# Second graph layer of a four-layer graph and expert network: row norms a further step later, and the values of three row tiles projected inside the attention

## The chip, the cores and the metric

The kernel runs on one core of one Trainium2 chip. The metric is the device time of one execution in microseconds (us), as the median of several runs; less is better. The engines are named as the profile names them: PE is TensorE's matmul, PEld its weight load, DVE is VectorE, ACT is ScalarE, POOL is GpSimd, SP is SyncE.

## What is computed

Four layers run one after the other on 1024 rows of 256 numbers, all in float32 unless said otherwise. Each layer is a graph step and then a mixture of experts, each added to `x`:

```python
x = x + gnn(layernorm(x), adj, ...)      # a different one in each layer
x = x + ffn(layernorm(x), ...)           # two of 16, 8, 8 or 16 experts a row
```

The change touches the graph step of the second layer (layer 1), an attention with 4 heads of 64 columns over a dense mask:

```python
h = (x @ W.T).reshape(n, 4, 64)                    # the values
e_src = einsum('nhd,hd->nh', h, a_src)
e_dst = einsum('nhd,hd->nh', h, a_dst)
e = leaky_relu(e_src[:, None, :] + e_dst[None, :, :], 0.2)
e = where(adj > 0, e, -inf)
out = einsum('ijh,jhd->ihd', softmax(e, axis=1), h).reshape(n, 256)
```

## The kernel before

The 1024 rows are 8 row tiles of 128 (`NT` is 8, `P` is 128, `D` is 256 in `DC` = 2 parts). Every stage is one block in which each engine has its own instruction list, written out in order; engines wait for each other by semaphores. A block ends when all engines have ended, and the next starts on all of them.

**The stage before the attention** is the end of the first layer's expert block, class `BeforeGraph1`. DVE sums a row tile, norms it twice (`summed`, `raised`, `norm`); PE turns it (`turn`, L196), ACT places the turned tile in `xnT` (`place`, L201), and PE projects it (`project`, L1004): the destination terms of 4 heads (L1012), the values (L1018), the source terms (L1020). ACT copies the three results out of PSUM in `keep` (L1030, L1033, L1034). PE's order is turn of tile t, then project of tile t-1. The weights' products stand in `w`, `wa`, `wab`; the values go to `V`.

**The attention** is `graph1` (L1093). It goes in 32 units; unit u is head u % 4 of row tile u // 4. For one unit:

- DVE: `mask` (L443) adds the mask row block to the destination terms and takes the row maximum, 128x1024;
- POOL: three small operations on 128x1 (L482, L483, L485) make two biases of the maximum; the third gives `biased`;
- ACT: `slope_of` (L498) applies slope and bias, 128x1024, and gives `sloped`;
- DVE: `shift` (L451) combines both branches into `lm`, 128x1024;
- PE: `turn` (L537) transposes `lm` in 8 parts; ACT: `exp_of` (L507) takes the exponential in two halves; PE: `weigh` (L548) multiplies by `V`, 8 parts.

The orders are loops over a step u, the same number on each engine:

```python
DVE  step u: mask(u); shift(u-2); end(u-behind); vector_step(u)     # L462
POOL step u: three operations of unit u; pool_step(u)               # L479
ACT  step u: exp_of(u-3); slope_of(u); scalar_step(u)               # L516
PE   step u: turn(u-2); weigh(u-3); tensor_step(u)                  # L555
```

`behind` is 5 here. `end` does something for every fourth unit only: `finish` of a whole row tile (L1104 to L1106).

**Beside the attention** the norm and the gate logits of each finished row tile are worked into these steps by `attend` (L569) with the class `Front`: DVE takes the `moments` (L238 to L242), POOL takes the power (`invert`, L250), DVE writes the normed tile (`norm`, L187), PE turns it (L196), ACT places it (L201), PE makes the `logits` (L262), DVE ranks them (`rank`: L273, L281, L282). The step of each is counted from `done(t)` = 4t+8, where the moments of row tile t stand. With `wait` = `behind` - 4 = 1 they are, before the change: the power at step 4t+9, norm and turn at 4t+10 and 4t+11, place 4t+12, logits 4t+13, rank 4t+14. What falls behind the last step is done in `vector_end`, `tensor_end`, `scalar_end` and `pool_end`. The same function serves the first layer (behind 4, wait 0) and the fourth (behind 4, wait 0).

SP loads the gate's weights and stores the normed tiles in DRAM while this runs; POOL issues no DMA in this block.

Of the kernel before, what the change touches and what calls it, by code (L numbers as in the profile page):

```python
# [15 lines left out]
P = 128  # L16
N = 1024
NT = N // P
D = 256
# [7 lines left out]
def build(nc, A, out):  # L27
# [19 lines left out]
    with top:  # L47
# [361 lines left out]
        def attention(block, ph, heads, slope, lowest, rows, rest, values, width, finish,  # L409
# [81 lines left out]
            @block.scalar  # L491
            def _(act):

                def slope_of(u):
                    act.wait_ge(biased, u + 1)
                    if u >= 4:
                        act.wait_ge(shifted, u - 3)
                    nc.scalar.activation(t2[u % 4][:, :], g[u % 4][:, :], ACT.Identity, bias=b2[:, u:u + 1],  # L498
                                         scale=slope).then_inc(sloped, 1)

                def exp_of(u):
                    for hf in range(2):
                        act.wait_ge(turned, 2 * u + hf + 1)
                        if u >= 2 and hf == 0:
                            act.wait_ge(weighed, u - 1)
                        q = slice(hf * NT // 2, (hf + 1) * NT // 2)
                        nc.scalar.activation(pT[u % 2][:, q, :], tp[u % deep][:, q, :], ACT.Exp)\  # L507
                            .then_inc(exped, 1)

                ahead = 1  # L510
                slope_of(0)
                if "scalar_early" in extra:
                    slope_of(1)
                    extra["scalar_early"](act)
                    ahead = 2
                for u in range(ahead, units + 3):  # L516
                    if u >= 3:
                        exp_of(u - 3)
                    if u < units:
                        slope_of(u)  # L520
                    if "scalar_step" in extra:
                        extra["scalar_step"](u, act)
                if "scalar_end" in extra:
                    extra["scalar_end"](act)
# [42 lines left out]


        def attend(block, ph, front, heads, slope, lowest, rows, rest, values, width, finish, scores, done, free=0,  # L569
                   settle=None, more=(), group=1, behind=4):  # L570

            units = NT * heads
            wait = behind - 4

            def normed(t):
                return done(t) + 1 + wait
# [88 lines left out]

            def pool_step(u, pool):
                for t in range(NT):  # L670
                    if done(t) + wait == u:
                        front.invert(pool, t)

            def pool_end(pool):
                for t in range(NT):
                    if done(t) + wait >= units:
                        front.invert(pool, t)

            def sync(sp):
# [3 lines left out]
            hooks = {"vector_step": vector_step, "vector_end": vector_end, "tensor_step": tensor_step,  # L683
                     "tensor_end": tensor_end, "scalar_step": scalar_step, "scalar_end": scalar_end,
                     "pool_step": pool_step, "pool_end": pool_end, "sync": sync}
            for name in ("tensor", "scalar_early"):
                if name in more:
                    hooks[name] = more[name]
            attention(block, ph, heads, slope, lowest, rows, rest, values, width, finish, scores, hooks, group, behind)
# [234 lines left out]


        class BeforeGraph1(Handover):
            H, DH, SLOPE = 4, 64, 0.2
            base = xn


# [73 lines left out]
            def project(self, pe, t):  # L1004
                H = self.H
                q = slice(t * P, (t + 1) * P)
                pe.wait_ge(self.norm.xnT_ready, t + 1)
                if t >= 2:
                    pe.wait_ge(self.columns_kept, t - 1)
                for h in range(H):  # L1010
                    for c in range(DC):
                        ins = nc.tensor.matmul(self.pd[t % 2][:, h, :], self.wab[:, c, h, :], xnT[:, c, q],  # L1012
                                               start=(c == 0), stop=(c == DC - 1))
                ins.then_inc(self.columns, 1)
                if t >= 2:
                    pe.wait_ge(self.values_kept, t - 1)
                for c in range(DC):
                    nc.tensor.matmul(self.pv[t % 2][:, 0:D], xnT[:, c, q], self.w[:, c, :], start=(c == 0), stop=(c == DC - 1))  # L1018
                for c in range(DC):
                    ins = nc.tensor.matmul(self.pv[t % 2][:, D:D + H], xnT[:, c, q], self.wa[:, c, :],  # L1020
                                           start=(c == 0), stop=(c == DC - 1))
                ins.then_inc(self.valued, 1)

            def scalar(self, act):
                H, DH, SLOPE = self.H, self.DH, self.SLOPE
                nc.scalar.activation(spent[:, :], power[:, 0, :], ACT.Exp)

                def keep(t):
                    act.wait_ge(self.columns, t + 1)
                    nc.scalar.activation(self.dst[:, :, t * P:(t + 1) * P], self.pd[t % 2][:, :, :], ACT.Copy)\  # L1030
                        .then_inc(self.columns_kept, 1)
                    act.wait_ge(self.valued, t + 1)
                    nc.scalar.activation(self.rest[:, t, :], self.pv[t % 2][:, D:D + H], ACT.Copy, scale=1.0 - SLOPE)  # L1033
                    nc.scalar.activation(self.V[:, t, :, 0:DH], self.pv[t % 2][:, 0:D].rearrange("p (h d) -> p h d", h=H),  # L1034
                                         ACT.Copy).then_inc(self.values_kept, 1)
                for t in range(NT + 1):
                    if t < NT:
                        self.norm.place(act, t)
                    if t >= 1:
                        keep(t - 1)  # L1040
# [52 lines left out]
        def graph1(before, gate_of):  # L1093
            H, DH, SLOPE = before.H, before.DH, before.SLOPE
            rest, dst, V = before.rest, before.dst, before.V
            with Phase("g1") as ph:
                r, part = ph.sb("r", [P, NT, H, 1]), [ph.sb(f"part{n}", [P, H, DH]) for n in range(2)]
                tp = ph.ps("front_tp", [P, DC, P])
                psl = ph.ps("front_psl", [P, NT, gate_of[0]])
                front = Front(ph, *gate_of, [tp[:, :, :]], psl, raised_here=range(NT))  # L1100
                block = ph.block()

                def finish(t, dve, link, o, gm):
                    link(nc.vector.reciprocal(r[:, t, :, :], o[:, :, DH:DH + 1]))  # L1104
                    link(nc.vector.tensor_tensor(part[t % 2][:, :, :], o[:, :, 0:DH], bc(r[:, t, :, :], [P, H, DH]), ALU.mult))
                    return nc.vector.tensor_tensor(x[:, t, :], x[:, t, :], part[t % 2][:, :, :].rearrange("p h d -> p (h d)"),  # L1106
                                                   ALU.add)

                attend(block, ph, front, H, SLOPE, lambda u: False, lambda u: dst[:, u % H, :],
                          rest[:, :, :].rearrange("p t h -> p (t h)"),  # L1110
                          lambda u, c: V[:, c, u % H, :], DH + 1, finish, None, lambda t: (t + 1) * H + 4, group=H, behind=5)


        class BeforeGraph2(Handover):
# [1120 lines left out]
```

## Time and profile before

| what | value |
| --- | --- |
| median of 3 runs | 1093.96 us (1091.34 to 1099.96) |
| the profiled execution's own time | 1096.7 us |
| its span, first to last instruction | 1094.8 us |
| PE busy | 956.3 us (87%) |
| PEld busy | 896.3 us (82%) |
| DVE busy | 701.8 us (64%) |
| ACT busy | 514.7 us (47%) |
| POOL busy | 445.4 us (41%) |
| attention of layer 1, first mask to last moments | 252.16 to 365.5 us |

The span is what the profiler saw between the first and the last instruction; the profiled execution took 1.9 us more than its span and 2.7 us more than the median. Busy time says how long an engine worked, not whether the others waited for it. The trace gives for each instruction its start, its duration and what ended the idle time before it.

### The profile page before, as it was taken

To read this page: it belongs to the slowest core of one execution; us is meant where nothing else is said; L and a number is where in the kernel's file an instruction comes from. 1 tells how busy PE (TensorE), PEld (TensorE's weight loads), DVE (VectorE), ACT (ScalarE), POOL (GpSimd) and SP (SyncE) were. 2 spreads that over 40 slices of the span, in tenths; PEclk is the share of its full clock that TensorE was granted. 3 is DMA by queue.
4 is the path that set the end of the run, shared out by engine and by line. 5 is a ranking of instruction groups with operands and counts; after the bars stand their busy time and mean duration, and the time that the engine had idled before them with its cause. 6 is when DMAs were issued, how large, how long until landed. Compare 5 with 4: busy or idle time off the path is not lost. (4 is left out here: it accounts for less than half of the span.)

```text
span 1094.8 us, 22761 instructions
## 1 busy us (share of the span) xinstructions
PE 956.3 (87%) x7554; PEld 896.3 (82%) x7554; DVE 701.8 (64%) x1653; ACT 514.7 (47%) x1001; POOL 445.4 (41%) x470
## 2 busy tenths in 40 slices
PE   6884999896899589989989899999889985999992
PEld 5584999786888579978979899999758875999992
DVE  3786777666899557776544466655656864666664
ACT  1252777134666357712045577767234532444341
POOL 1152577426776147621200145551244521344441
PEclk8797999798999789979989999999899995999997
DMA  7007865300000437322450011168200007655954
GB/s 250 2 25 241 312 219 178 97 1 1 11 10 11 183 109 269 135 83 95 129 195 8 16 35 38 38 220 308 92 2 5 11 21 268 255 168 172 322 162 135
DMA packets 57675, 132.30 MB, mean 121 GB/s; under 512 B 9664, under 2 KB 35712, under 8 KB 52864
## 3 DMA queue, kind: packets, MB, share of 16 engines
q1 hardware_dynamic: 47376, 106.45, 27.7%
q0 software_dynamic: 9024, 24.65, 7.4%
q8 instruction: 43, 0.70, 0.3%
q10 hardware_dynamic: 1200, 0.23, 0.1%
q14 instruction: 32, 0.26, 0.1%
HBM read 191.97 MB, written 17.56 MB: 191 GB/s over the span
## 5 line engine op out<-in xcount | busy, mean ns | idle before, releaser
L1959 PE MATMUL r_pH<-e_xsT,e_w 128*128 128x128 f32 x2304 | 281.5, 280 | 10.0 <-DVE e_xsT L2072 5.0
L1959 PEld LDWEIGHTS r_pH<-e_xsT,e_w 128*128 128x128 f32 x2304 | 272.4, 197 | 12.8 <-issue 9.6
L1914 POOL DMA_INDIRECT y_rows<-e_ys,e_to x94 | 156.8, 1668 | 190.6 <-DVE e_ys L2102 95.5
L1924 POOL DMA_INDIRECT e_xs<-xn_rows,e_idx x94 | 103.4, 1100 | 161.7 <-DVE e_idx L2076 120.4
L2088 DVE TENSOR_TENSOR e_w_lo<-e_w,e_w_hi 128x1024 fp32r<-128x1024 f32 (+1 forms) x74 | 113.4, 1532 | 13.8 <-ACT e_w_hi L2030 12.7
L1974 PE MATMUL r_pY<-e_w_hi,e_h_hi 128*128 128x256 f32 x384 | 114.5, 298 | 2.2 <-issue 2.2
L2030 ACT ACTIVATE e_w_hi<-e_w 128x1024 fp32r<-128x1024 f32 (+1 forms) x74 | 96.0, 1298 | 27.7 <-DMA e_w<-w_in 22.4
L498 ACT ACTIVATE g_t<-g_g,g_small 128x1024 f32<-128x1024 f32 x56 | 64.1, 1150 | 94.8 <-POOL g_small L485 94.8
L1974 PE MATMUL r_pY<-e_w_lo,e_h_hi 128*128 128x256 f32 x384 | 108.4, 282 | 0.0
L1974 PE MATMUL r_pY<-e_w_hi,e_h_lo 128*128 128x256 f32 x384 | 108.4, 282 | 0.0
L451 DVE SCALAR_TENSOR_TENSOR g_lm<-g_g,g_small,g_t 128x1024 f32<-128x1024 f32 x56 | 71.6, 1280 | 9.5 <-ACT g_t L498 7.0
L537 PE MATMUL g_tp<-ident,g_lm 128*128 128x128 f32 x448 | 62.8, 286 | 16.7 <-DVE g_lm L451 16.0
L1974 PEld LDWEIGHTS r_pY<-e_w_hi,e_h_hi 128*128 128x128 f32 x384 | 73.3, 191 | 2.7 <-issue 2.6
L482 POOL TENSOR_SCALAR g_small<-g_small,n_rest 128x1 f32<-128x1 f32 x48 | 49.5, 1032 | 59.1 <-DVE g_small L443 58.5
L1974 PEld LDWEIGHTS r_pY<-e_w_lo,e_h_hi 128*128 128x128 f32 x384 | 73.5, 191 | 0.0
L1974 PEld LDWEIGHTS r_pY<-e_w_hi,e_h_lo 128*128 128x128 f32 x384 | 73.2, 191 | 0.0
L537 PEld LDWEIGHTS g_tp<-ident,g_lm 128*128 128x128 f32 x448 | 53.0, 149 | 23.6 <-DVE g_lm L451 21.0
L2042 ACT ACTIVATE xnT<-r_pH,e_w 128x128 f32<-128x128 f32 x176 | 50.2, 368 | 44.2 <-PE r_pH L1959 39.0
L548 PE MATMUL g_o<-n_V,g_pT 128*128 128x65 f32 x512 | 62.9, 277 | 5.4 <-ACT g_pT L507 5.3
L548 PEld LDWEIGHTS g_o<-n_V,g_pT 128*128 128x128 f32 x512 | 60.6, 194 | 8.5 <-ACT g_pT L507 7.7
L443 DVE CUSTOM_DVE_ANT_0 g_g<-n_dst,neg 128x1024 f32<-128x1024 f32 x48 | 58.1, 1217 | 13.9 <-PEq L2152 13.9
L179 POOL TENSOR_SCALAR mean_var<-mean_var 128x1 f32<-128x1 f32 x37 | 17.7, 478 | 120.6 <-DVE mean_var L239 81.8
(321 smaller groups left out, 1970.6 us busy)
## 6 DMA issues: line engine op xcount, KB each, us to landing
e_w<-w_in SPq DMA_DIRECT2D x56, 1024.0 KB
e_w<-w_in SPq DMA_DIRECT2D x84, 512.0 KB
e_w<-w_in SPq DMA_DIRECT2D x52, 514.0 KB
e_w<-w_in SPq DMA_DIRECT2D x24, 1028.0 KB
e_w<-y_rows SPq DMA_DIRECT2D x32, 256.0 KB, 5.4
p_adj<-adj_in SPq DMA_DIRECT2D x8, 512.0 KB, 11.3
xn_rows<-xn SPq DMA_DIRECT2D x32, 128.0 KB, 1.7
n_adjT<-adjT_in SPq DMA_DIRECT2D x8, 512.0 KB, 4.9
```

Of the source, the lines that this page charges most:

```text
L443: nc.vector.tensor_tensor_reduce(out=g[u % 4][:, :], in0=rows(u), in1=neg[:, u // heads, :], scale=1.0, scalar=-3e38, op0=ALU.add, op1=ALU ...
L451: nc.vector.scalar_tensor_tensor(out=lm[u % 2][:, :], in0=g[u % 4][:, :], scalar=b1[:, u:u + 1], in1=t2[u % 4][:, :], op0=ALU.add, op1=ALU ...
L498: nc.scalar.activation(t2[u % 4][:, :], g[u % 4][:, :], ACT.Identity, bias=b2[:, u:u + 1], scale=slope).then_inc(sloped, 1)
L537: ins = nc.tensor.transpose(tp[u % deep][:, c, :], lm[u % 2][:, c * P:(c + 1) * P], ident[:, :])
L548: ins = nc.tensor.matmul(o[k % 2][:, part, 0:width], pT[u % 2][:, c, :], values(u, c), start=(c == 0), stop=(c == NT - 1))
L1914: pool.indirect_dma_start(out=y_rows[:, :], in_=ys[b][:, :], in_offset=None, out_offset=bass.IndirectOffsetOnAxis(ap=to[b][:, :], axis=0))\
L1924: pool.indirect_dma_start(out=xs[b][:, :], out_offset=None, in_=xn_rows[:, :], in_offset=bass.IndirectOffsetOnAxis(ap=idx[b][:, :], axis=0))\
L1959: ins = nc.tensor.matmul(pH[b % 2][:, f, :], w1[b][:, at:at + P], xsT[b % 2][:, c, :], start=(c == 0), stop=(c == DC - 1))
L1974: ins = nc.tensor.matmul(pY[m][:, :], h[m][:, f, :], w[m][:, f * D:(f + 1) * D], start=(f == 0 and n == 0), stop=(f == FC - 1 and n == 2))
L2030: nc.scalar.activation(w2_hi[b % 2][:, :], w2[b][:, :], ACT.Copy).then_inc(w2_rounded, 1)
L2042: ins = nc.scalar.activation(hT[b % 2][:, f, :], pH[b % 2][:, f, :], function, bias=b1)
L2088: nc.vector.tensor_tensor(w2_lo[b % 2][:, :], w2[b][:, :], w2_hi[b % 2][:, :].bitcast(F32), ALU.subtract).then_inc(w2_split, 1)
```

## The change

Two things change in layer 1, and the first layer and the fourth keep their steps.

1. In `attend` the number `wait` is given by the caller: 2 for layer 1, 0 for the others. The power stays at step 4t+9 (`power_at` is min(wait, 1)); norm, turn, place, logits and rank of every row tile go one step later, to 4t+11, 4t+12, 4t+13, 4t+14 and 4t+15.
2. The values of row tiles 5, 6 and 7 are no longer projected by `project` and copied by `keep` before the attention. PE does it as its first work in the attention's block (`project` in `graph1`), and ACT copies them to `V` (`place`) ahead of `slope_of(0)`, by the new hook `scalar_first`. Each goes through one of two PSUM banks, `spare`, which afterwards serve as the front's turning space and as the space for the logits.

```diff
@@ attention
                 ahead = 1
+                if "scalar_first" in extra:
+                    extra["scalar_first"](act)
                 slope_of(0)
@@ attend
-                   settle=None, more=(), group=1, behind=4):
+                   settle=None, more=(), group=1, behind=4, wait=0):
...
-            wait = behind - 4
+            power_at = min(wait, 1)
 
             def normed(t):
                 return done(t) + 1 + wait
...
-                    if done(t) + wait == u:
+                    if done(t) + power_at == u:
                         front.invert(pool, t)
...
-                    if done(t) + wait >= units:
+                    if done(t) + power_at >= units:
                         front.invert(pool, t)
@@ BeforeGraph1
-            H, DH, SLOPE = 4, 64, 0.2
+            H, DH, SLOPE, EARLY = 4, 64, 0.2, 5
...
-                for c in range(DC):
-                    nc.tensor.matmul(self.pv[t % 2][:, 0:D], xnT[:, c, q], self.w[:, c, :], start=(c == 0), stop=(c == DC - 1))
+                if t < self.EARLY:
+                    self.values(self.pv[t % 2][:, 0:D], t)
...
+            def values(self, pv, t):
+                for c in range(DC):
+                    ins = nc.tensor.matmul(pv, xnT[:, c, t * P:(t + 1) * P], self.w[:, c, :], start=(c == 0), stop=(c == DC - 1))
+                return ins
+
+            def keep_values(self, pv, t):
+                return nc.scalar.activation(self.V[:, t, :, 0:self.DH], pv.rearrange("p (h d) -> p h d", h=self.H), ACT.Copy)
...
+                    ins = nc.scalar.activation(self.rest[:, t, :], self.pv[t % 2][:, D:D + H], ACT.Copy, scale=1.0 - SLOPE)
+                    if t < self.EARLY:
+                        ins = self.keep_values(self.pv[t % 2][:, 0:D], t)
+                    ins.then_inc(self.values_kept, 1)
@@ graph1
+                spare = [ph.ps(f"front{n}", [P, 512]) for n in range(2)]
+                late, late_kept = ph.sem("late"), ph.sem("late_kept")
+
+                def project(pe):
+                    for t in range(before.EARLY, NT):
+                        if t >= before.EARLY + 2:
+                            pe.wait_ge(late_kept, t - before.EARLY - 1)
+                        before.values(spare[t % 2][:, 0:D], t).then_inc(late, 1)
+                    pe.wait_ge(late_kept, NT - before.EARLY)
+
+                def place(act):
+                    for t in range(before.EARLY, NT):
+                        act.wait_ge(late, t - before.EARLY + 1)
+                        before.keep_values(spare[t % 2][:, 0:D], t).then_inc(late_kept, 1)
...
-                          lambda u, c: V[:, c, u % H, :], DH + 1, finish, None, lambda t: (t + 1) * H + 4, group=H, behind=5)
+                          lambda u, c: V[:, c, u % H, :], DH + 1, finish, None, lambda t: (t + 1) * H + 4,
+                       more={"tensor": project, "scalar_first": place}, group=H, behind=5, wait=2)
```

## Rows read from the trace of the kernel before

**Rows 1.** Waits of DVE, 252 to 370 us: who waited for whom, us, times, longest

```profile
DVE xn L187 <- POOL rstd L250: 6.3, 7, 1.0
DVE lg L273 <- PE g_front_psl L262: 5.7, 2, 3.6
DVE g_lm L451 <- ACT g_t L498: 5.1, 3, 1.9
```

**Rows 2.** Timeline of one row tile (start, duration, engine, line): DVE, POOL, ACT, steps 16 to 19

```profile
296.74 0.41 DVE L187 TENSOR_SCALAR xn<-x,mean_var,rstd 128x256 f32<-128x256 f32 x1 [0.97 <-POOL rstd L250]
...
305.89 0.38 ACT L201 ACTIVATE xnT<-g_front_tp 128x256 f32<-128x256 f32 x1
...
306.15 1.09 ACT L507 ACTIVATE g_pT<-g_tp 128x512 f32<-128x512 f32 x2
...
306.57 1.22 DVE L443 CUSTOM_DVE_ANT_0 g_g<-n_dst,neg 128x1024 f32<-128x1024 f32 x1
...
307.72 1.28 DVE L451 SCALAR_TENSOR_TENSOR g_lm<-g_g,g_small,g_t 128x1024 f32<-128x1024 f32 x1
307.94 1.21 POOL L483 TENSOR_SCALAR g_small<-g_small 128x1 f32<-128x1 f32 x1
309.23 0.19 POOL L485 TENSOR_TENSOR g_small<-g_small,n_rest 128x1 f32<-128x1 f32 x1
...
309.97 0.42 DVE L187 TENSOR_SCALAR xn<-x,mean_var,rstd 128x256 f32<-128x256 f32 x1 [0.97 <-POOL rstd L250]
...
310.85 1.21 DVE L443 CUSTOM_DVE_ANT_0 g_g<-n_dst,neg 128x1024 f32<-128x1024 f32 x1
```

**Rows 3.** Timeline of steps 7 and 8, before the first norm: DVE, POOL and PE

```profile
270.99 1.28 DVE L451 SCALAR_TENSOR_TENSOR g_lm<-g_g,g_small,g_t 128x1024 f32<-128x1024 f32 x1
...
271.21 2.27 POOL L483 TENSOR_SCALAR g_small<-g_small 128x1 f32<-128x1 f32 x1
...
272.19 1.22 DVE L443 CUSTOM_DVE_ANT_0 g_g<-n_dst,neg 128x1024 f32<-128x1024 f32 x1
...
274.97 1.29 DVE L451 SCALAR_TENSOR_TENSOR g_lm<-g_g,g_small,g_t 128x1024 f32<-128x1024 f32 x1 [1.55 <-ACT g_t L498]
...
275.47 0.77 PE L548 MATMUL g_o<-n_V,g_pT 128*128 128x65 f32 x5 [0.56 <-ACT g_pT L507]
```

**Rows 4.** Timeline of the stage's end (row tile 5, then 7) and the attention's first mask

```profile
242.15 1.03 PE L1018 MATMUL e_pv<-n_w,xnT 128*128 128x256 f32 x4
...
243.02 0.50 PE L1020 MATMUL e_pv<-n_wa,xnT 128*128 128x4 f32 x4
...
249.92 0.17 ACT L1033 ACTIVATE n_rest<-e_pv 128x4 f32<-128x4 f32 x1 [0.61 <-PE e_pv L1020]
249.99 0.38 ACT L1034 ACTIVATE n_V<-e_pv 128x256 f32<-128x256 f32 x1
...
252.16 1.23 DVE L443 CUSTOM_DVE_ANT_0 g_g<-n_dst,neg 128x1024 f32<-128x1024 f32 x1 [12.44 <-PEq L2152]
```

**Rows 5.** ACT's first slopes; then a window: us, busy PE, PEld, DVE, ACT, POOL, PEclk, DMA

```profile
256.45 2.19 ACT L498 ACTIVATE g_t<-g_g,g_small 128x1024 f32<-128x1024 f32 x2 [6.08 <-POOL g_small L485]
...
253.00:254.00 1.00, 0.00 (x0) 0.00 (x0) 1.00 (x3) 0.00 (x0) 0.49 (x1) 1.00 0.17 10
```

**Rows 6.** Timeline of the attention's end: last shift, turn, weigh, logits and finish

```profile
355.93 1.28 DVE L451 SCALAR_TENSOR_TENSOR g_lm<-g_g,g_small,g_t 128x1024 f32<-128x1024 f32 x1
...
358.48 1.04 PE L537 MATMUL g_tp<-ident,g_lm 128*128 128x128 f32 x8
...
359.36 1.90 PE L548 MATMUL g_o<-n_V,g_pT 128*128 128x65 f32 x16
...
361.09 0.56 PE L262 MATMUL g_front_psl<-g_front_gw,xnT 128*128 128x8 f32 x4
...
361.51 1.98 PE L548 MATMUL g_o<-n_V,g_pT 128*128 128x65 f32 x16
...
363.53 0.18 DVE L1104 RECIPROCAL g_r<-g_o 128x4 f32<-128x4 f32 x1 [1.19 <-PE g_o L548]
```

More of the change, by code:

```diff
@@ L685, in attend @@
                      "pool_step": pool_step, "pool_end": pool_end, "sync": sync}
-            for name in ("tensor", "scalar_early"):
+            for name in ("tensor", "scalar_early", "scalar_first"):
                 if name in more:
@@ L1032, in keep @@
                     act.wait_ge(self.valued, t + 1)
-                    nc.scalar.activation(self.rest[:, t, :], self.pv[t % 2][:, D:D + H], ACT.Copy, scale=1.0 - SLOPE)
-                    nc.scalar.activation(self.V[:, t, :, 0:DH], self.pv[t % 2][:, 0:D].rearrange("p (h d) -> p h d", h=H),
-                                         ACT.Copy).then_inc(self.values_kept, 1)
+                    ins = nc.scalar.activation(self.rest[:, t, :], self.pv[t % 2][:, D:D + H], ACT.Copy, scale=1.0 - SLOPE)
+                    if t < self.EARLY:
+                        ins = self.keep_values(self.pv[t % 2][:, 0:D], t)
+                    ins.then_inc(self.values_kept, 1)
                 for t in range(NT + 1):
@@ L1097, in graph1 @@
                 r, part = ph.sb("r", [P, NT, H, 1]), [ph.sb(f"part{n}", [P, H, DH]) for n in range(2)]
-                tp = ph.ps("front_tp", [P, DC, P])
-                psl = ph.ps("front_psl", [P, NT, gate_of[0]])
-                front = Front(ph, *gate_of, [tp[:, :, :]], psl, raised_here=range(NT))
+                spare = [ph.ps(f"front{n}", [P, 512]) for n in range(2)]
[10 more added lines that the diff above has]
+                        before.keep_values(spare[t % 2][:, 0:D], t).then_inc(late_kept, 1)
+                front = Front(ph, *gate_of, [spare[0][:, 0:DC * P].rearrange("p (c q) -> p c q", q=P)],
+                              spare[1][:, 0:NT * gate_of[0]].rearrange("p (t e) -> p t e", e=gate_of[0]), raised_here=range(NT))
                 block = ph.block()
```

## Prediction, made before the changed kernel was run

> **What bounds the kernel now.** I read the engine totals, then the windows of 200 to 370 us, the waits of each engine in the attention, and last the timeline there, instruction by instruction. The totals do not help: PE is busy 87% of the span, but in the changed stretch PE waits and DVE sets the pace. The waits of DVE show three things: it waits for POOL's power before the norm of 7 row tiles, 6.3 us together; three times for a slope, 5.1 us; twice, at the end, for logits [rows 1]. The first is what moving the norm addresses.
>
> The timeline of one row tile shows the period: norm to norm 309.97 - 296.74 = 13.23 us [rows 2]. DVE goes on with its next instruction 1.20 us after a shift starts, so it could have begun at 307.72 + 1.20 = 308.92; the norm starts at 309.97, 1.05 us late. The period is 12.18 us of DVE work and this wait. From the second finished row tile on it repeats unchanged, six times (row tiles 0 to 5; tile 6 waits 0.46 us).
>
> The reader should then look at POOL beside DVE. Its three operations of a unit are 128x1 and take 0.2 to 0.4 us when DVE is idle or small, but L483 at 307.94 takes 1.21 us: it ends 0.15 us after the shift, when DVE has stopped to wait for the norm [rows 2]. L485 follows at once, in that same pause, and the slope of unit 17 can start. So the wait of 1.05 us is also the gap through which POOL gets its result out. What happens without such a gap stands in the steps before the first norm: L483 starts 0.22 us behind a shift, exactly as at 307.94, but a mask follows the shift without a pause; now it takes 2.27 us, until that mask has ended too. The next shift, which needs the slope, comes 274.97 - 272.19 = 2.78 us after that mask, against 307.72 - 306.57 = 1.15 when nothing is missing: DVE stands still for 1.63 us [rows 3]. The same pattern stands once more at 262.54 us, with 1.56 us of waiting by the trace's own count.
>
> **The change, part by part.**
>
> *Values out of the stage before.* The last three row tiles there are PE's: DVE has ended its last norm at 239.7 us and PE works through projections without a gap. From the start of the value matmuls to the start of the next group is 243.02 - 242.15 = 0.87 us [rows 4], three times 2.61 us; tiles 5, 6 and 7 are just the three that PE does back to back. Nothing takes the place: the copies PE waits for (the destination terms, the turned tile) lie over 1 us ahead of its need even at the shorter pace. ACT's last copy goes as well: its end at 249.99 + 0.38 = 250.37 becomes the end of L1033, 249.92 + 0.17 = 250.09 [rows 4], 0.28 us. The attention's first mask came 1.79 us after ACT's end and keeps this distance. Gain 2.89 us; 2.6 if PE's end decides the block's end, 3.1 with the matmuls' full 1.03 us each.
>
> *Values into the attention.* PE does the three tiles from the block's start, ACT copies each in 0.38 us. PE needs 3 x 0.87 = 2.6 us, the last copy ends at about 3.1 us. ACT's first slope starts 256.45 - 252.16 = 4.29 us after the first mask, since POOL's first operation is held up by three masks, and PE's first turn comes later still [rows 4, 5]. So the work is hidden, with 1.2 us to spare: cost 0. The cover is the granted clock: it reads 1.00 until 254 us, 4 us after PE's last matmul in the old stage [rows 5], and PE now pauses about 2 us only. Were it at half, 1.2 GHz, the matmuls would take 5.2 us and the first slope would be 1.1 to 1.9 us late, with the whole attention behind it. The semaphore waits of PE and ACT hold up nothing else, as both wait here for POOL anyway. A turn at a higher clock in the first units gains nothing, since POOL and DVE bound there.
>
> *Norm and what follows, a step later.* Take row tile 2 and lay the new order on rows 2. Until the shift of unit 16 at 307.72 all is as before. Then:
> 1. No norm stands in step 18, so mask 19 starts at 308.92 instead of 310.85. POOL's L483 of unit 17, started at 307.94, sees the shift followed by a mask, the case of rows 3: it ends at 310.2 instead of 309.15. Then L485, slope 17, and only then shift 17: at 308.92 + 2.78 = 311.70, which is 1.63 us later than DVE could.
> 2. Norm 2 stands behind this shift, at 312.90. The power has long been there (POOL takes it in the pause), so the old wait of 1.05 us is gone. The norm takes 0.33 us to the next instruction.
> 3. Then rank 1, now in step 19. It needs logits 1, which stand in PE's step 18 behind weigh 15, behind the exponential of unit 15, which ACT issues behind slope 17, the late one. In rows 3 weigh starts 275.47 - 274.97 = 0.50 us after the late shift. Here place 1 stands between, which has moved to the same step: 306.15 - 305.89 = 0.26 us [rows 2]. So weigh 15 at 312.46; a weigh takes 1.73 us to the next, logits 0.56 us [rows 6]: ready at 314.75, and DVE is there at 313.23. It waits 1.55 us, with the semaphore. Then rank takes 0.55 and mask 20 starts.
> In the finish and in this second pause POOL catches up, so the next step's slopes are in time, and the pattern starts again.
>
> Period: 12.18 + 1.63 + 1.55 = 15.36 us against 13.23, that is 2.13 us more for each row tile. Counted over the attention: shift waits at units 9, 13, 17, 21, 25, 29, six times 1.63 = 9.8 us; rank waits for row tiles 0 to 4, five times 1.55 = 7.75 us; removed, six norm waits of 1.05 = 6.3 us. The last shift is 11.2 us later. I laid all 32 units out in this way, all engines in order; the old order laid out so puts the last finish within 0.2 us of the trace, and the new one gives 11.1.
>
> Bounds: the shift wait lies between 0, if L483 got through at the shift's end, and the 1.9 us of the largest such wait [rows 1]; the two cases with the same neighbours say 1.56 and 1.63. The rank wait lies between 0 and the 3.6 us at the end [rows 1]; it is worked out from ACT's and PE's written order.
>
> *The end.* Before, PE was behind: the last shift ended at 357.21 and its turn started at 358.48, and from shift end to the end of the last weigh it was 363.49 - 357.21 = 6.28 us, with logits 5 between [rows 6]. Now PE has caught up: turn 0.97, two weighs of 1.73 make 4.5 us, 1.75 less. But logits 5 now follow the last weigh, and rank 5 stands ahead of the last finish on DVE: 0.56 + 0.55 = 1.1 us, which nothing hides, since everything after hangs on this finish. The norm of tile 6 is early in either order. Sum of the end: -0.65 us.
>
> Sum for the attention: 11.2 - 0.65 = 10.6 us; with the stage before, 10.6 - 2.9 = **+7.7 us**. What follows the attention starts later by as much, and its work is the same. The profiled execution would take 1096.7 + 7.7 = 1104.4 us; it stood 2.7 us above the median, so for the median 1093.96 + 7.7 = **1101.7 us**.
>
> The Trainium skill, SBUF — State Buffer, section Who interferes with whom, says that a DVE instruction with two SBUF inputs and a GpSimd instruction that reads SBUF exclude each other, and the second blocks until the first has finished. The trace agrees that it blocks, but one POOL instruction lasted through two DVE instructions, 2.27 us [rows 3]. By the page alone L483 would end with the shift and L485 would be caught by mask 19: the slope comes some 0.1 us earlier, and the sum is 1 us less, an estimate by that page.
>
> **The rivals.**
>
> A. *It works as meant.* POOL gets through at the shift's end though a mask follows; L485 also slips in before mask 19. Then the norm waits go, 6.3 us, no rank is late, and with the 2.9 us it is -9.2: 1084.8 us. For it: every such row in the steady part is short (1.21 us). Against it: in all of them DVE is idle or in small operations behind the shift, and both cases without that took 2.27 us. It decides if L483 stays at 1.2 us and L485 at 0.2. This is the case on the other side.
>
> B. *The shift wait comes, the rank wait does not*, because the exponential is ready earlier than I take it. Then 9.8 - 6.3 = 3.5, the end -0.65, the stage before -2.9: about 0, 1093.9 us. Against it: ACT's order is fixed, exponential u-3 behind slope u-1.
>
> C. *The placed values delay the first slope*, at half clock: 1.1 to 1.9 us more, some 1103.2 us. Against it: the clock's row above. A similar price, up to 2 us, would come if PE in its longer pauses (up to 2.2 us) fell to the lower clock for a while; nothing in this trace fell in so short a pause.
>
> **How the numbers follow.** Forecast 0.68, A 0.10, B 0.12, C 0.10. About 1% of the time, 10.9 us, is what a measurement of this kernel can tell from no change (three runs lay 8.6 us apart). Slower by more begins at 1104.9 us: a part of C, and of the forecast what the runs' own spread carries over it, together 0.18. Faster by more begins below 1083.0: less than half of A, 0.04. The rest is 0.78. The range goes from 1089, which takes in B and its spread and leaves out A, to 1107, which takes in C and both waits at 1.9 us; about 0.18 is left out.
>
> **What would show it.** Right: the wait of the norm for POOL is gone; in its place DVE waits for ACT's slope about 8 or 9 times (now 3), near 15 us in sum, and for the logits (L273) some 7 times, 8 us or more beside the last ones. Six more L483 rows at about 2.27 us. First mask near 249.3 us. Norm to norm 15.4 us. PE idle ahead of weigh 2 us once a row tile. L1104's last start follows rank 5 directly. Wrong: a period near 12.2 us with L483 still at 1.2 us (A), a period near 13.8 (B), or a first slope later than 4.3 us behind the first mask (C).

## The result, and the profile after

The changed kernel takes 1107.13 us, the median of 4 runs (1102.55 to 1112.86), the kernel before 1093.88 beside it: ratio 1.012, 95% interval 1.0085 to 1.0155, or +13.2 us where +7.7 was forecast. It is slower, for the reasons forecast and one more. The time lies just outside the range, 0.13 us above its upper end. In the timelines below, rows that stand between those shown are left out.

Waits of DVE in the changed attention, 248 to 378 us (us in total, times, longest), where before had [rows 1]:

```profile
DVE lg L273 <- PE g_front L262: 18.1, 6, 4.5
DVE g_lm L451 <- ACT g_t L498: 14.4, 9, 1.9
DVE xn L187 <- POOL rstd L250: 0.5, 1, 0.5
```

The wait of the norm for the power is gone but for one, as the change meant. The wait for the slope has come nine times instead of three, as forecast. The wait for the logits was to be some 8 us beside the last; it is 18.1 - 4.5 = 13.6 us.

The pattern of one row tile, timeline with PE's clock up (steps 13 to 15; start, duration, engine, line):

```profile
291.00 2.27 POOL L483 TENSOR_SCALAR g_small<-g_small 128x1 f32<-128x1 f32 x1
291.98 1.22 DVE L443 CUSTOM_DVE_ANT_0 g_g<-n_dst,neg 128x1024 f32<-128x1024 f32 x1
293.35 0.19 POOL L485 TENSOR_TENSOR g_small<-g_small,n_rest 128x1 f32<-128x1 f32 x1
294.75 1.29 DVE L451 SCALAR_TENSOR_TENSOR g_lm<-g_g,g_small,g_t 128x1024 f32<-128x1024 f32 x1 [1.55 <-ACT g_t L498]
295.53 2.00 PE L550 MATMUL g_o<-n_V,g_pT 128*128 128x65 f32 x16 [2.05 <-ACT g_pT L507]
295.97 0.40 DVE L187 TENSOR_SCALAR xn<-x,mean_var,rstd 128x256 f32<-128x256 f32 x1
297.97 0.17 DVE L273 TENSOR_TENSOR lg<-g_front,g_front_gb 128x8 f32<-128x8 f32 x1 [1.59 <-PE g_front L262]
```

This is the forecast's pattern in its own numbers. L483, 1.21 us in [rows 2], now lasts 2.27 us as in [rows 3]; it ends with the mask, L485 and the slope follow, and the shift starts 294.75 - 291.98 = 2.77 us behind the mask. The norm stands right behind it, with no wait, and the rank waits 1.59 us, because the weighing ahead of its logits started late. PE paused 2.05 us.

Then comes what was not in the sum. Windows of the same stretch (busy PE, PEld, DVE, ACT, POOL, granted clock, DMA), and PE's and DVE's rows in it:

```profile
300.00:305.00 5.00, 3.64 (x32) 3.27 (x31) 4.83 (x10) 2.12 (x3) 2.70 (x4) 1.00 0.01 2
305.00:310.00 5.00, 4.73 (x23) 4.73 (x23) 3.70 (x6) 0.93 (x1) 4.72 (x6) 0.52 0.00 0
310.00:315.00 5.00, 5.00 (x26) 5.00 (x25) 1.62 (x2) 4.51 (x8) 2.07 (x5) 0.50 0.09 30
...
325.00:330.00 5.00, 5.00 (x29) 5.00 (x29) 3.41 (x5) 2.54 (x5) 4.74 (x7) 0.59 0.00 0
330.00:335.00 5.00, 5.00 (x48) 5.00 (x48) 1.56 (x6) 3.85 (x6) 0.57 (x3) 1.00 0.09 30
```

```profile
305.27 1.97 PE L539 MATMUL g_tp<-ident,g_lm 128*128 128x128 f32 x8 [1.23 <-DVE g_lm L451]
307.04 3.51 PE L550 MATMUL g_o<-n_V,g_pT 128*128 128x65 f32 x16
311.47 0.40 DVE L187 TENSOR_SCALAR xn<-x,mean_var,rstd 128x256 f32<-128x256 f32 x1
316.36 0.17 DVE L273 TENSOR_TENSOR lg<-g_front,g_front_gb 128x8 f32<-128x8 f32 x1 [4.49 <-PE g_front L262]
329.88 0.41 DVE L187 TENSOR_SCALAR xn<-x,mean_var,rstd 128x256 f32<-128x256 f32 x1
333.66 0.17 DVE L273 TENSOR_TENSOR lg<-g_front,g_front_gb 128x8 f32<-128x8 f32 x1 [3.37 <-PE g_front L262]
347.16 0.40 DVE L187 TENSOR_SCALAR xn<-x,mean_var,rstd 128x256 f32<-128x256 f32 x1
```

PE paused 2.05, 0.40 and 1.23 us between its groups; then the granted clock fell from 1.00 to 0.50 (2.4 to 1.2 GHz) and stayed there for some 24 us, although PE was now busy throughout. A turn takes 1.97 instead of 1.04 us, a weighing 3.51 instead of 1.90 [rows 6], and the rank waits of DVE are 4.49 and 3.37 us. The five inside the attention are 1.59, 4.49, 3.37, 1.59 and 2.50 us, 13.5 together. Norm to norm is 15.50 us where the rank between them waits 1.59 us (295.97 to 311.47), and 18.41 and 17.28 where it waits 4.49 and 3.37.

At the stage's end and the attention's start:

```profile
248.04 2.83 PE L1028 MATMUL g_front<-n_w,xnT 128*128 128x256 f32 x12 [2.11 <-PEq L2177]
248.08 1.23 DVE L443 CUSTOM_DVE_ANT_0 g_g<-n_dst,neg 128x1024 f32<-128x1024 f32 x1 [9.73 <-PEq L2177]
250.90 0.39 ACT L1032 ACTIVATE n_V<-g_front 128x256 f32<-128x256 f32 x1 [0.48 <-PE g_front L1028]
252.36 1.15 ACT L498 ACTIVATE g_t<-g_g,g_small 128x1024 f32<-128x1024 f32 x1 [1.08 <-POOL g_small L485]
```

The first mask comes 10.14 us behind the last norm of the stage before; it was 12.85. The last value is copied at 251.29 and the first slope starts 4.28 us behind the mask, as before (4.29, [rows 4, 5]).

Two measures serve below. The **stretch** runs from the attention's first mask to the end of its last moments: 113.3 us before, 130.3 after. The **low clock** is what one-microsecond windows of it show, each counted as 2 x (1 - granted clock), from 12 us behind the first mask on, since PE starts at the lower level in every kernel, to some 2 us before the stretch's end: 0.8 us before, 31.5 after. This count also takes in a first rise that comes late, which is no fall; a table at the end of the experiments tells the two apart. Stretch (+17.0) and stage end (-2.7) make +14.2; the profiled pair differs by 10.6 only, since the other stages, which the change does not touch, took 3.6 us less in it. "Laid out" means all engines' instructions in written order with the durations of the rows, at the full clock; it gives 113.4 for before and 124.1 for after. So 6.2 us of the changed stretch are to be explained, and the clock is the suspect.

### The profile page after: what moved, and what is told of

It is laid out like the page before. It is cut to its first block and busy times, and to the rows that moved or that the text cites. A ratio compares the mean times of both kernels' runs of the same rounds, so it can differ in the third digit from the quotient of the medians.

```text
span 1105.4 us, 22762 instructions
## 1 busy us (share of the span) xinstructions
PE 965.5 (87%) x7554; PEld 904.9 (82%) x7554; DVE 702.4 (64%) x1653; ACT 515.4 (47%) x1001; POOL 448.2 (41%) x470
## 3 DMA queue, kind: packets, MB, share of 16 engines
q1 hardware_dynamic: 47376, 106.45, 27.3%
## 5 line engine op out<-in xcount | busy, mean ns | idle before, releaser
L2113 DVE TENSOR_TENSOR e_w_lo<-e_w,e_w_hi 128x1024 fp32r<-128x1024 f32 (+1 forms) x74 | 113.5, 1534 | 13.2 <-ACT e_w_hi L2055 12.2
L539 PE MATMUL g_tp<-ident,g_lm 128*128 128x128 f32 x448 | 68.7, 304 | 15.1 <-DVE g_lm L451 14.4
L539 PEld LDWEIGHTS g_tp<-ident,g_lm 128*128 128x128 f32 x448 | 58.7, 161 | 22.2 <-DVE g_lm L451 15.2
L550 PE MATMUL g_o<-n_V,g_pT 128*128 128x65 f32 x512 | 70.4, 298 | 6.5 <-ACT g_pT L507 6.4
L550 PEld LDWEIGHTS g_o<-n_V,g_pT 128*128 128x128 f32 x512 | 69.5, 218 | 7.7 <-ACT g_pT L507 7.7
L507 ACT ACTIVATE g_pT<-g_tp 128x512 f32<-128x512 f32 x112 | 60.6, 594 | 12.9 <-PE g_tp L539 12.8
```

What stands on the lines that cost most here:

```text
L539: ins = nc.tensor.transpose(tp[u % deep][:, c, :], lm[u % 2][:, c * P:(c + 1) * P], ident[:, :])
L550: ins = nc.tensor.matmul(o[k % 2][:, part, 0:width], pT[u % 2][:, c, :], values(u, c), start=(c == 0), stop=(c == NT - 1))
L2113: nc.vector.tensor_tensor(w2_lo[b % 2][:, :], w2[b][:, :], w2_hi[b % 2][:, :].bitcast(F32), ALU.subtract).then_inc(w2_split, 1)
```

## The experiments

**The two parts apart.** Values early alone, norms where they were; and norms later alone, with all eight value tiles in the stage before and nothing placed in the attention:

```
e1:  - group=H, behind=5, wait=2)      + group=H, behind=5, wait=1)
e2:  - EARLY = ... 5                   + EARLY = ... 8
```

> Only the values of row tiles 5 to 7 move into the attention; norms, logits and ranks stay at their old steps. The stretch read is from DVE's first mask to its last moments (113.3 us before, 130.3 us changed). Theory T (DVE loses by the steps of norm and rank alone; the moved values are hidden): the stretch stays 113.3 within 0.3 us, the first mask comes 2.9 us earlier relative to DVE's last norm of the old stage, the time falls by 2.9 us to a ratio of about 0.997. Rival R1 (the values in the attention, their PSUM banks or their copies ahead of the first slope cost part of the loss): the stretch is several us longer than 113.3 and the time is not below before.

> Only the norms and all behind them go a step later; all values are projected before the attention as before. T: shift waits of about 1.55 us at six units and rank waits of 1.6 us or more at five, a stretch of 124.2 us if TensorE's granted clock stays at its upper level, and up to 130 us where it falls as in the changed kernel; first mask at its old distance. R1: the stretch is near 113.3 or below, since the values are not there. The intended effect (norm waits gone, nothing in their place) would give 107 us.

Values alone: 1091.90 us (10 runs), ratio 0.9981 (0.9960 to 1.0002), stretch 113.84, low clock 0.0. Norms alone: 1114.86 us (one run), stretch 135.4, low clock 37.5, rank waits up to 8.2 us; this stretch is 5 us over the 130 expected, as the clock fell three times instead of twice, and the third time the last rank waited 8.2 us. The loss is all in the norms. In the profile of the first, PE happened to be at the lower level when it did the placed values:

```profile
246.94 4.51 PE L1028 MATMUL g_front<-n_w,xnT 128*128 128x256 f32 x12 [2.11 <-PEq L2177]
251.49 0.38 ACT L1032 ACTIVATE n_V<-g_front 128x256 f32<-128x256 f32 x1 [1.11 <-PE g_front L1028]
251.77 3.22 ACT L498 ACTIVATE g_t<-g_g,g_small 128x1024 f32<-128x1024 f32 x3
```

4.51 us against 2.83: the first slope comes 4.79 us behind the mask, 0.5 late. That is rival C in small; it is not what made the change slow.

**PE's pause filled.** The changed kernel, with 26 small matmuls (into an unused part of PSUM, issued by the helper `rouse`) ahead of the weighing that waits 2 us; then the same kernel timed:

```
+ def pause(u):
+     if 10 <= u < NT * H and u % H == 2:
+         rouse(spare[1][:, 3 * P:4 * P], 26)
```

> The changed kernel, and in PE's long pause (ahead of weigh in step 4t+10) 26 small bf16 matmuls into an unused part of a PSUM bank, 1.4 us of the 2 us. T with the clock as second cause: the granted clock stays at its upper level from 265 us on, the rank waits are 1.6 us each in place of 1.6 to 4.5, shift waits unchanged at 1.55, the stretch 124.2 us, so some 6 us shorter than the changed kernel's 130.3. Rival R2 (the clock falls for another reason than PE's pauses, or it costs nothing since DVE bounds): dips remain or the stretch stays near 130.

> The kernel of e3 again, now timed: the changed kernel with 26 small matmuls in PE's long pause. One look gave a stretch of 125.1 us and one short fall of the clock. T: with the clock held up most of the time the loss is that of the written order alone, 10.6 - 2.9 = 7.7 us, and what short falls are left add under 1.5 us: time 1102 us, ratio 1.006 to 1.009, clearly under the changed kernel's 1.012. R2 (the clock's falls cost nothing in the time): ratio 1.012 as before the filling.

```profile
302.69 1.09 PE L539 MATMUL g_tp<-ident,g_lm 128*128 128x128 f32 x8 [1.22 <-DVE g_lm L451]
...
306.23 1.61 PE L144 MATMUL g_front<-ones_b 128*128 128x128 bf16 x26
308.44 2.00 PE L550 MATMUL g_o<-n_V,g_pT 128*128 128x65 f32 x16 [0.60 <-ACT g_pT L507]
```

The pause shrinks from 2.05 to 0.60 us and nothing useful is added, yet in the first execution the stretch is 125.1 us and the low clock 8.0: four of the five rank waits are 1.59 to 1.60, one 1.99. The laid out 124.1 is nearly met. Timed, it is 1102.49 us (4 runs), ratio 1.0095 (1.0065 to 1.0125); the profile of that run shows 17.7 us at the lower level and a stretch of 129.2. Of the 17.7 us, 10.8 are the first rise, which came 22 us behind the first mask instead of 13: DVE waited there for two turns, and its first norm comes 2.0 us later than in e3's profile. Only 6.8 us are a fall, at 309.3, right behind the other pause, 1.22 us before a turn, which is left unfilled; the rank behind it waits 4.05 us. Both profiles of this kernel thus show one fall of 6.8 us, the changed kernel's two falls of 30.7 together. The ratio is below the changed kernel's 1.0120, but the intervals overlap: that the time gains by the filling is not shown, the gain in the clock is.

**PE's pauses alone.** The reverse: norms and ranks in the old order, values early, and unused DVE work behind the shift of steps 9, 11, up to 29, that makes PE wait longer.

```
+ for n in range(4):
+     nc.vector.bn_stats(out=gap[...], in_=before.w[:, 0, :])
- wait=2)                     + wait=1)
```

> The kernel with the early values and the norms and ranks of the kernel before (whose stretch was 113.8 us with no lowered clock), with PE's pauses alone made longer: four unused statistics of VectorE, about 1.4 us, behind the shift of every second step from 9 to 29, eleven times, so that PE waits that much longer for the next shifted tile. Nothing of the order of norms and ranks is changed. Theory (the granted clock falls where PE's pauses reach 1.2 to 2.2 us): more than 15 us of the stretch at the lower level, and a stretch over the 123 to 129 us that eleven times 1.35 us on 113.8 give with up to six times 1.0 us of norm waits absorbed. Rival (the clock fell with the later norms and ranks, or by chance, and PE's pauses have nothing to do with it): under 5 us at the lower level, stretch 123 to 129 us.

PE's rows, then windows:

```profile
289.10 1.09 PE L539 MATMUL g_tp<-ident,g_lm 128*128 128x128 f32 x8 [1.32 <-DVE g_lm L451]
...
303.87 1.97 PE L539 MATMUL g_tp<-ident,g_lm 128*128 128x128 f32 x8 [1.45 <-DVE g_lm L451]
305.63 3.52 PE L550 MATMUL g_o<-n_V,g_pT 128*128 128x65 f32 x16
```

```profile
300.00:305.00 5.00, 3.55 (x29) 3.42 (x28) 4.86 (x12) 2.76 (x5) 2.62 (x6) 0.86 0.00 2
305.00:310.00 5.00, 5.00 (x25) 5.00 (x25) 2.84 (x6) 2.90 (x4) 1.82 (x4) 0.50 0.09 30
310.00:315.00 5.00, 5.00 (x25) 5.00 (x25) 4.93 (x12) 2.34 (x3) 1.70 (x3) 0.50 0.00 0
```

Low clock 32.0 us, against 0.0 for the same order without the pauses; stretch 130.4, 1102.32 us (one run). No norm or rank moved, so the rival that ties the clock to their order falls; e1 and e2 show that it is not the moved values either. The pause at 289.10 left the clock up and the like one at 303.87 did not: a pause of this length makes the fall possible, not certain. Longer pauses and less work for PE in each us come together here, and this run can't tell which of the two counts.

**The ranks later.** The rank waits for logits placed only one step before it; `rank_at = logits_at(k) + lag` moves it by `lag` steps. First lag 3 in the changed kernel:

```
- return logits_at(k) + 1             + return logits_at(k) + lag
```

> The changed kernel with every rank two further steps later (step 4t+17), behind the shift that before had only a mask behind it. T: the logits are long there, so no rank waits inside the steps; the 0.55 us of small DVE work now stands in a stretch of masks and shifts and lets POOL catch up, so the shift waits at units 17, 21, 25, 29 shrink from 1.55 to 0.3 us or less; PE's pauses stay under 0.5 us and the clock stays up. Stretch 110.6 us, the time 1094 - 2.9 - 2.7 = 1088, ratio 0.995. If only the rank waits matter and POOL's hold-up is no matter of small work behind a shift, the stretch is 116 to 117 us and the ratio about 1.000.

1097.80 us (10 runs), ratio 1.0027 (1.0001 to 1.0054). No rank waits are left inside the attention, where they took 13.5 us, and the stretch is 8.5 us shorter; but it is 121.8, not 110.6, with a low clock of 32.0 us, 27.3 of it in two falls, one right behind the pause of 2.05 us that this order keeps. DVE now waits for PE's turns (7.9 us, 6 times) and weighings (7.6, 5 times) instead. The expectation of the stretch missed by the clock, which I had taken to matter only for the rank waits, and by something that e8 shows without it.

**Ranks later and pauses filled**, lag 2 (as e3, `lag=2`), lag 3 (fills in steps 4, 7, 10 and 14), and lag 2 timed:

> The changed kernel with every rank one more step later (step 4t+16), where the logits have been ready, and 26 small matmuls in PE's pause. T: the rank waits vanish, five times 1.6 us, the shift waits of 1.55 at six units stay; the last rank no longer stands ahead of the last finish: stretch 116.8 us if the clock holds (124.1 - 7.4). If the rank waits were only the place where another delay shows, the time comes back in the finish or a mask and the stretch stays near 124.

> The kernel of e4 (ranks in step 4t+17) with small matmuls in PE's pauses of the first steps (26 each in steps 4, 10 and 14, 8 in step 7). e4's stretch was 121.8 us, with the clock at its lower level for some 15 us early and 10 us late. T: with the early pauses filled the clock holds and the stretch is the 110.6 to 111.5 us of the written order; time 1094 - 2.9 - 2.5 = 1088.6, ratio 0.995. R2 (falls of the clock have nothing to do with PE's pauses): a stretch of 115 us or more again, ratio 1.00.

> The kernel of the one look at 1088.29 us again, timed: norms at 4t+11, ranks two steps behind the logits (4t+16), 26 or fewer small matmuls ahead of the weighing at the pause. Theory: rank waits stay gone and the shift waits of 1.2 to 1.55 us stay; stretch 116.8 us by the written order, so 1094 - 2.7 + 3.5 = 1094.8 at most and 1088 to 1095 over runs, ratio 0.995 to 1.001. Rival (the clock falls as in the unfilled kernels): stretch over 122 us, time over 1099.

Lag 2: stretch 116.7 us with a low clock of 5.1, as laid out (116.8), 1088.29 us in one run; timed 1092.46 (10 runs), ratio 0.9984 (0.9956 to 1.0012), and there 118.9 with 10.6. In both profiles all of this is the late first rise: with the rank waits gone and the pause filled PE never waits over 0.60 us behind it, and the clock never falls. Lag 3: 1090.66 us (12 runs), ratio 0.9976 (0.9954 to 0.9998), stretch 116.6 and not 110.6. The low clock is 14.2 us, 7.4 of it the first rise; the rest is two falls of 3.4 us behind pauses of 1.45 us in steps that were not filled, and DVE waits for PE in neither. What made the stretch longer is mainly this:

```profile
308.19 1.28 DVE L451 SCALAR_TENSOR_TENSOR g_lm<-g_g,g_small,g_t 128x1024 f32<-128x1024 f32 x1
308.49 1.14 POOL L483 TENSOR_SCALAR g_small<-g_small 128x1 f32<-128x1 f32 x1
309.39 0.41 DVE L187 TENSOR_SCALAR xn<-x,mean_var,rstd 128x256 f32<-128x256 f32 x1
309.72 1.26 POOL L485 TENSOR_TENSOR g_small<-g_small,n_rest 128x1 f32<-128x1 f32 x1
312.19 1.28 DVE L451 SCALAR_TENSOR_TENSOR g_lm<-g_g,g_small,g_t 128x1024 f32<-128x1024 f32 x1 [1.26 <-ACT g_t L498]
```

The later rank freed the step that the expectation named, but behind the norm of the same row tile L483 passes and L485 is held by the next mask, so that the shift after it waits. That comes four times, 1.25 to 1.33 us each, 5.1 us together, and e4 has two of them.

**The held POOL instruction.** If L483 is caught because a mask follows the shift at once, some DVE work in between that leaves POOL alone must let it through. One statistic of 0.43 us behind the shift of step 4t+10, then two, with 12 small matmuls in PE's pause:

```
+ nc.vector.bn_stats(out=gap[...], in_=before.w[:, 0, :])
+ rouse(spare[1][:, 3 * P:4 * P], 12)
```

> The changed kernel with one idle-making DVE instruction (a bn_stats of 0.43 us with one input, result unused) behind the shift of step 4t+10, where only a mask followed, and 12 small matmuls in PE's pause. T (POOL's operation passes as soon as a shift is followed by something that is not a mask): L483 at units 9, 13, 17, 21, 25, 29 takes 1.2 us in place of 2.27, the shift waits there fall from 1.55 to about 0.15 us though DVE has 0.43 us more to do, rank waits stay 1.6: stretch 118.2 us if the clock holds, 5.9 us shorter than 124.1 by an added instruction. Rival (the shift is late for another reason, ACT's order or POOL's own speed): shift waits stay 1.1 to 1.55 and the stretch is 124 to 127 us.

> The changed kernel with 0.8 us of unused VectorE work (two statistics of one weight slice) directly behind the shift of step 4t+10, and 12 small matmuls in PE's pause. Theory (GpSimd's bias add of that unit is held through two back-to-back instructions of VectorE, and the exact gap in which all three of its operations pass was 0.34 us too short with one statistic): L483 1.2 us and L485 0.2 us in these units, the seven 1.55 us shift waits fall under 0.3 us, rank waits 1.5 us stay; stretch 119.7 us with the clock up, against 124.1 for the changed kernel laid out by the same order with the clock up. Rival (the shift waits come from PE or ScalarE, not from the held GpSimd): the shift waits stay over 1.0 us and the stretch is 124.1 plus six times 0.8, 129 us.

With one, POOL shows:

```profile
304.96 1.21 POOL L483 TENSOR_SCALAR g_small<-g_small 128x1 f32<-128x1 f32 x1
306.25 1.27 POOL L485 TENSOR_TENSOR g_small<-g_small,n_rest 128x1 f32<-128x1 f32 x1
```

L483 is through, but L485 starts just as the mask does and is caught in turn: the shift wait only falls to 1.25, where 0.15 was expected. So this expectation failed: the stretch is 128.2 us and not 118.2, with 17.1 us at the lower clock in two falls and a rank wait of 4.34 us in it, and the run took 1101.58 us. With two, 0.74 us:

```profile
305.55 1.21 POOL L483 TENSOR_SCALAR g_small<-g_small 128x1 f32<-128x1 f32 x1
306.85 0.19 POOL L485 TENSOR_TENSOR g_small<-g_small,n_rest 128x1 f32<-128x1 f32 x1
```

One shift wait of 1.26 us follows the first such gap (behind the norm at 281.47, where L485 is caught again); behind the five later ones none is left. Four of the five rank waits stay at 1.53 to 1.54 us (one 2.64, with the clock down), and the stretch is 120.7 us (119.7 expected, low clock 8.7), the one run 1096.11 us. Against e3, with a like low clock and the same waits otherwise (125.1 us), unused DVE work makes the stretch 4.4 us shorter, as expected: the shift waits are POOL's, and what frees it is a gap in which L483 and L485 both find room.

**A version meant to beat both**: values early, norms at their old step, so that PE's pauses stay short, and ranks later.

```
- group=H, behind=5, wait=2)          + group=H, behind=5, wait=1, lag=4)
```

> The early values are kept (first mask 2.7 us sooner behind the last norm of the stage before), the norms stay at the step of the kernel before, 4t+10, and the ranks go to 4t+17 instead of 4t+14. Theory (the waits come from the written order; the clock falls only where PE's pauses lengthen): no shift waits 1.55 us (they came only with the norm's step), the six norm waits of about 1.0 us stay, the rank waits go, PE's pauses stay as in the kernel before, so the granted clock stays at 1.00 in the attention. Laid out by the written order from row durations the stretch from first mask to last moments is 110.1 us (before 113.3, after 130.3). Sum: 1094 - 2.7 - 3.2 = 1088.1, ratio 0.9946. Rival (a late rank lets the clock fall by itself, as in the run with the norms at their new step and ranks at 4t+17): over 15 us of the stretch at the lower level, stretch 116 to 121 us, time 1094 to 1099.

1091.28 us (12 runs), ratio 0.9977 (0.9955 to 0.9999). PE never paused over 0.73 us between 264 and 355 us and the clock did not fall there, so the rival is out, but the stretch is 112.6 us, not 110.1. DVE's norms:

```profile
290.09 0.42 DVE L187 TENSOR_SCALAR xn<-x,mean_var,rstd 128x256 f32<-128x256 f32 x1 [0.98 <-POOL rstd L250]
303.00 0.41 DVE L187 TENSOR_SCALAR xn<-x,mean_var,rstd 128x256 f32<-128x256 f32 x1 [0.45 <-POOL rstd L250]
315.91 0.41 DVE L187 TENSOR_SCALAR xn<-x,mean_var,rstd 128x256 f32<-128x256 f32 x1 [0.46 <-POOL rstd L250]
```

The period is 12.91 us, 0.32 less than before, as the norm waits halve; one shift near the end waits 1.26 us, and the last finish waits 5.04 us for PE. Next to the values alone (0.9981) it is no clear gain: all of the versions at 0.998 are within a fraction of a per cent of the kernel before, and none is shown to be better than another.

**The clock in all profiles.** Times in us; a fall is counted only behind the first rise, as is PE's longest pause (with the clock up).

| run | stretch | low clock | of it in falls | falls | longest pause |
| --- | --- | --- | --- | --- | --- |
| before | 113.3 | 0.8 | 0 | 0 | 0.73 |
| changed | 130.3 | 31.5 | 30.7 | 2 | 2.05 |
| e1 | 113.8 | 0.0 | 0 | 0 | 1.16 |
| e2 | 135.4 | 37.5 | 37.5 | 3 | 2.06 |
| e3 | 125.1 | 8.0 | 6.8 | 1 | 1.23 |
| e5 (kernel of e3) | 129.2 | 17.7 | 6.8 | 1 | 1.23 |
| e4 | 121.8 | 32.0 | 27.3 | 2 | 2.05 |
| e6 | 128.2 | 17.1 | 17.1 | 2 | 1.41 |
| e7 | 116.7 | 5.1 | 0 | 0 | 0.60 |
| e11 (kernel of e7) | 118.9 | 10.6 | 0 | 0 | 0.60 |
| e8 | 116.6 | 14.2 | 6.8 | 2 | 1.45 |
| e9 | 112.6 | 4.9 | 0 | 0 | 0.73 |
| e10 | 120.7 | 8.7 | 3.4 | 1 | 1.29 |
| e12 | 130.4 | 32.0 | 30.7 | 2 | 1.45 |

In this stretch each of the nine profiles with more than one pause of 1.2 us or longer has a fall, and none of the five others has one. Outside the stretch the clock fell at shorter ones too, as rows below show.

## Why the prediction was right in sign and short in size

1. *Stage before, -2.89.* Right: -2.71 by the first mask.
2. *Placed values, 0.* Right in this profile. In e1 they cost 0.5 us at the lower clock, below the 1.1 to 1.9 of rival C: the matmuls took 4.51 us there and not 5.2.
3. *Six shift waits of 1.63.* Right: six new ones of 1.55 to 1.59 us by the trace's count, about 1.62 with the semaphore. The held L483 as their cause is shown by e6 and e10. Rival A fell: each L483 that started 0.2 us into a shift with a mask behind it lasted 2.27 us.
4. *Six norm waits removed.* Right.
5. *Five rank waits of 1.55.* **This is the term that failed.** Where the clock was up they were 1.59, as worked out from ACT's and PE's written order, and rival B fell. But the text took PE's durations from rows with the clock up and gave the lower clock "up to 2 us", since "nothing in this trace fell in so short a pause". From 264 to 355 us that trace had no pauses of this kind at all: its PE never waited more than 0.73 us. And outside that stretch the reading is wrong. Two us behind the attention the clock of the kernel before fell behind pauses of 0.56 and 1.76 us, about where the next one, of 0.57 us, began:

```profile
364.28 0.58 PE L262 MATMUL g_front_psl<-g_front_gw,xnT 128*128 128x8 f32 x4 [0.56 <-ACT xnT L201]
366.63 0.44 PE L196 MATMUL g_front_tp<-ident,xn 128*128 128x128 f32 x2 [1.76 <-DVE xn L187]
367.63 1.00 PE L262 MATMUL g_front_psl<-g_front_gw,xnT 128*128 128x8 f32 x4 [0.57 <-ACT xnT L201]
```

```profile
366.00:367.00 1.00, 0.37 (x2) 0.20 (x2) 0.46 (x2) 0.00 (x0) 0.12 (x1) 1.00 0.00 0
367.00:368.00 1.00, 0.43 (x3) 0.40 (x3) 0.00 (x0) 0.38 (x1) 0.00 (x0) 0.59 0.38 131
```

It fell in the same way at 558.3 us, behind pauses of 0.84 and 0.39 us. These rows were at hand, and show the clock falling at pauses shorter than the 2.2 us of rival C. The change itself made pauses of 2.05 and 1.23 us, the clock fell for 30.7 us of the stretch, and the five waits took 13.5 us instead of 7.75, +5.8. With it the sum is 7.7 + 5.8 = 13.5. The 13.2 between the medians is that near in part by luck; the sizes to compare are those of the traces, where the stretch was to grow by 10.6 + 5.8 = 16.4 and grew by 17.0.
6. *The end, -0.65.* Right but for the size: from the last shift to the moments 9.17 us instead of 9.56, -0.39.
7. *Period 15.36.* 15.50; the same in e3 with the clock up all the while (293.38 to 308.88).

The clock is shown as the cause of the 6 us from both sides: filling a pause takes the falls from 30.7 to 6.8 us in both profiles (e3, e5), filling it with the rank waits gone leaves none (e7, e11), and lengthening pauses in the old order brings them (e12). The rank waits inside the attention grow beyond 1.7 us only in periods with a fall, in which PE's rows take nearly twice as long, or at once behind one. All this is read from traces; the times alone don't show it. Without it the change would still lose 6 to 8 us: laid out, 124.1 - 113.4 - 2.7 = 8.0, and e3's one run with little of it took 1099.87, 5.8 us over the kernel before. What stays open is which pause tips the clock, whether its length or PE's smaller share of work counts, and how much of the time varies by it: only one of the four runs of the changed kernel has a trace, and with mean clocks of 0.919, 0.906, 0.919 and 0.908 they took 1107.28, 1112.86, 1102.55 and 1106.99 us.

## What to carry to other kernels

A wait that one engine makes can be the gap through which another gets its result out; before removing it, look for rows on the other engine that end inside it. When a change lengthens TensorE's pauses, price its work behind them at the lower clock too, and look through the whole trace of before, not only the changed stretch, for the shortest pauses behind which the clock fell. And put consumers (here the rank) far enough behind their producers that one late link doesn't stop the engine that sets the pace.

## What the hardware showed unexpectedly

The clock fell with PE busy for most of the time: 3.64 of 5 us in the changed kernel's window at 300, 3.55 of 5 in e12's, with no single pause over 2.05 us in the one and 1.45 in the other. It then stayed down for some 24 us of nearly unbroken work in the one and 14 in the other. The Trainium skill, TensorE: Matmul & The Clock Gate, section A second HAM failure mode: psum-queue depth-cycling, tells of a kernel that cycles through PSUM banks, in which frequent short idle times between groups of matmuls make the clock swing. The rows here agree as to the swing (granted clock 1.00, then 0.50 for 24 us, then 1.00); here the pauses come from another engine's late results.

Whether GpSimd's L483 is held through one DVE instruction or two depends on when it starts. In the nine profiles before, changed, e3, e4, e6, e8, e9, e10 and e12, all 30 that started 0.2 us into a shift with a mask right behind it lasted 2.27 us, to the mask's end. The 18 that started within 0.05 us of the shift's start lasted 1.33 to 1.35 us, to the shift's end, although a mask followed too (changed kernel):

```profile
262.21 1.28 DVE L451 SCALAR_TENSOR_TENSOR g_lm<-g_g,g_small,g_t 128x1024 f32<-128x1024 f32 x1 [1.56 <-ACT g_t L498]
262.22 1.34 POOL L483 TENSOR_SCALAR g_small<-g_small 128x1 f32<-128x1 f32 x1
263.41 1.22 DVE L443 CUSTOM_DVE_ANT_0 g_g<-n_dst,neg 128x1024 f32<-128x1024 f32 x1
```

The reading "a mask follows, so L483 takes 2.27 us" needs this second condition; in the new order it was met in all six periods. L483 also passes if only 0.4 us of DVE work that reads a single large tile lies between (1.21 us behind a statistic in e6, 1.14 behind a norm in e8). The next POOL instruction, L485, is then the one that is held, for 1.26 to 1.27 us; in none of the nine profiles was it held through two.
